# A fused graph network, linear attention and routed expert kernel on one Trainium2 core: the routed stage reads rows of sums, eight at a time, and its up product takes high and low halves side by side

## The reference

```
xn = _layernorm(x)
x  = x + gnn(xn, edges)                 # two graph convolutions, relu between
       + mix(xn)                        # linear attention over all nodes, projection, layer norm
x  = x + ffn(_layernorm(x))

def ffn(xt):                            # xt: 3125 x 768
    probs = softmax(xt @ router_w.T)    # 8 experts
    top_w, top_i = top_k(probs, 2)
    e_sel = max(top_i)                  # one expert for each row
    out = silu(xt @ W1[e_sel]) @ W2[e_sel]      # 768 -> 128 -> 768
```

## Time and profile before

| | us |
|---|---|
| median of 3 runs | 2436.15 (2434.61 to 2436.8) |
| the profiled execution's own time | 2431.91 |
| its span, first to last instruction | 2430.2 |
| PE busy in the span | 2332.9 (96%) |
| DVE, ACT, POOL busy | 1256.0, 865.0, 864.6 |

### The profile page before, as it was taken

The page is one execution under the profiler, slowest core; times in us unless marked ns, Lnnn a source line. Parts: engine busy times, 40 slices in busy tenths (PEclk is TensorE's granted clock), DMA queues, the critical chain, the costliest instruction groups (busy, mean ns, idle before and its releaser), DMA issues.

```text
span 2430.2 us, 44796 instructions
## 1 busy us (share of the span) xinstructions
PE 2332.9 (96%) x16783; PEld 1585.1 (65%) x16783; DVE 1256.0 (52%) x2843; ACT 865.0 (36%) x1323; POOL 864.6 (36%) x615
## 2 busy tenths in 40 slices
PE   5999999999999999999999999999999999999597
PEld 3878787878666666676666666666665566666375
DVE  6757575735667676765214344434431444444444
ACT  3546464634737373552113222222220111111143
POOL 1001216567777787776630111111100000000166
PEclk9999999999999999999999999999999999999899
DMA  7788876654332313234337867766745465554287
GB/s 287 276 282 286 264 274 156 180 130 81 66 64 3 66 0 65 19 34 111 47 55 235 241 208 210 232 216 205 220 167 198 146 216 182 190 189 152 76 180 141
DMA packets 172421, 385.63 MB, mean 159 GB/s; under 512 B 74800, under 2 KB 81818, under 8 KB 166396
## 3 DMA queue, kind: packets, MB, share of 16 engines
q1 hardware_dynamic: 90220, 313.83, 37.6%
q0 software_dynamic: 71264, 40.45, 15.4%
q10 hardware_dynamic: 10800, 29.50, 3.1%
HBM read 222.76 MB, written 166.44 MB: 160 GB/s over the span
## 4 chain that ended last, share of the span: by engine, by line
PE 79%; DVE 7%; ACT 7%; issue 4%; DMA 2%; SPq 1%; POOL 0%; DVEq 0%; ACTq 0%; POOLq 0%
PE pair L1899 33%; PE pair L393 31%; PE pair L1715 5%; PE pair L1695 2%; PE pair L1645 2%; DVE arena L1349 2%; DVE arena L1351 2%; DVE arena L1355 2%; ACT arena L950 2%; PE pair L1704 1%; ACT arena L879 1%; PE pair L1819 1%; DMA arena<-hl_dram,arena 1%; ACT arena L960 1%; ACT arena L886 1%
## 5 line engine op out<-in xcount | busy, mean ns | idle before, releaser
L393 PE MATMUL pair<-arena 128*128 128x384 f16 (+3 forms) x5760 | 894.4, 316 | 5.3 <-issue 3.4
L747 POOL DMA_INDIRECT cells<-arena x392 | 658.5, 1680 | 566.6 <-DMA cells<-arena 426.3
L1899 PE MATMUL pair<-arena 128*128 128x384 f16 x4900 | 814.2, 326 | 0.9 <-DVE arena L1516 0.9
L393 PEld LDWEIGHTS pair<-arena 128*128 128x128 f16 x5760 | 564.7, 98 | 318.0 <-issue 7.6
L1899 PEld LDWEIGHTS pair<-arena 128*128 128x128 f16 x4900 | 474.1, 98 | 306.8 <-issue 2.4
L779 POOL DMA_INDIRECT slots<-arena x25 | 28.8, 1150 | 484.7 <-DVEq L1571 452.1
L1715 PE MATMUL pair<-arena 128*128 128x66 f32 x1200 | 157.1, 274 | 4.2 <-ACT arena L921 3.9
L1715 PEld LDWEIGHTS pair<-arena 128*128 128x128 f32 x1200 | 145.9, 192 | 13.1 <-ACT arena L921 10.5
L921 ACT ACTIVATE arena<-pair,arena 128x256 f32<-128x256 f32 x300 | 124.0, 472 | 68.3 <-PE pair L1695 65.8
L1023 ACT ACTIVATE arena<-arena 128x768 f32<-128x768 f32 x25 | 23.4, 935 | 333.8 <-DVE arena L1450 333.8
L765 POOL DMA_DIRECT2D arena<-cells x25 | 30.3, 1213 | 284.7 <-DMA arena<-cells 278.1
(11 more groups left out here) (202 smaller groups left out, 2441.4 us busy)
## 6 DMA issues: line engine op xcount, KB each, us to landing
cells<-arena SPq DMA_DIRECT2D x50, 800.0 KB, 9.5
ahl_dram<-arena SPq DMA_DIRECT2D x23, 1600.0 KB, 10.9
arena<-ahl_dram SPq DMA_DIRECT2D x23, 1600.0 KB, 8.0
arena<-in_x SPq DMA_DIRECT2D x70, 384.0 KB, 3.8
arena<-key_dram SPq DMA_DIRECT2D x28, 896.0 KB, 5.7
arena<-cells SPq DMA_DIRECT2D x25, 800.0 KB, 7.5
arena<-cells POOLq DMA_DIRECT2D x25, 800.0 KB, 7.7
split_w<-arena SPq DMA_DIRECT2D x32, 384.0 KB
```

What stands on the lines that cost most here:

```text
L393: ins = nc.tensor.matmul(dst[half], left(k, a), right(k, b, half), start=start and n == 0, stop=stop and n == 2)
L747: nc.gpsimd.indirect_dma_start(cells[k], bass.IndirectOffsetOnAxis(ap=idx_all[:, m:m + 1], axis=0), val_all[:, m:m + 1], None, bounds_chec ...
L1899: ins = nc.tensor.matmul(pair[u][:, half, 0:HD], a[:, 0, s * P:(s + 1) * P], X[part][:, s, half * HD:(half + 1) * HD], start=(s == 0 and p ...
```

## The change

- `z_out` becomes 770 wide (`ZW`): the row of sums, then the shift and the scale of its layer norm. Layer 2 stores these rows to `z_rows` alone, in place of the store to the output and the one to `hl_dram`. The cast on ACT and `low` on DVE are gone.
- The router turns float32 rows: 6 float32 transposes with a float32 identity (`turn32`) in place of 12 float16 ones. ACT then copies the high halves out, and DVE subtracts them from PSUM for the low ones, behind ACT. The router of tile `T-2` is moved into the products of tile `T-1`.
- The routed stage gathers rows of sums (eight buffers), ACT normalises each with the shift and scale of its row (`rows_normal`), PE turns them in float32, ACT copies the high half out, and DVE subtracts (`rows_evict`).
- `up` has 6 products of 256 columns (high and low halves side by side, `fT`) and 6 of 128. The two halves of the result are added on DVE (`add_halves`) before silu reads them. `down` uses one pair of PSUM banks, so it waits for the result before it.
- The result is added to the gathered row on DVE and written to the output rows without adding in memory. A buffer of gathered rows is thus free only after the result.
- The table is made one tile a partition; PE reads 24 of the 32 expert numbers before the stage's first transposes (`READ_FIRST`). POOL clears the gather buffers before the last tile's slots.

```diff
-NG, NO = 6, 4
+NG, NO = 8, 4
+ZW = D + 2
+READ_FIRST = 24
...
             def layer2(n, u, i):
-                act.wait_ge(out_ev, n + 1)
-                act.dma_start(out[bass.ds(tile_at(n) * P, P), :], z_out[u]).then_inc(out_st[u], 16)
                 if reused(n):
                     route_evict(n - 1)
                 act.wait_ge(var_ready, C + n + 1)
                 nc.scalar.activation(lnb[:, u, 0:1], lnb[:, u, 1:2], ACT.Sqrt).then_inc(sd_ready, 1)
                 act.wait_ge(xn_ready, T + n + 1)
-                if reused(i):
-                    act.wait_ge(xn_st[u], 16 * (13 - u) + 16 * i)
-                    act.wait_ge(tr_done, n - 1)
-                nc.scalar.copy(fhl[u][:, 0:D], fn).then_inc(hi_ready, 1)
-                act.wait_ge(lo_ready, T + n + 1)
-                act.dma_start(hl_dram[bass.ds(tile_at(n) * P, P), :], fhl[u]).then_inc(xn_st[u], 16)
+                act.dma_start(z_rows[bass.ds(tile_at(n) * P, P), :], z_out[u]).then_inc(out_st[u], 16)
...
+            def rows_normal(j):
+                q = j % NG
+                act.wait_ge(gathered[q], gathered_base[q] + 16 * (j // NG) + 16)
+                if j >= 2:
+                    act.wait_ge(g_tr, j - 1)
+                nc.scalar.activation(gx[j % 2], g_in[q][:, 0:D], ACT.Identity, bias=g_in[q][:, D:D + 1],
+                                     scale=g_in[q][:, D + 1:D + 2]).then_inc(f_norm, 1)
...
             for j in range(FT):
+                if j + 3 < FT:
+                    rows_normal(j + 3)
                 if j + 2 < FT:
                     rows_evict(j + 2)
                 if j + 1 < FT:
                     silu(j + 1)
...
             def rows_evict(j):
-                dve.wait_ge(g_tr, j + 1)
-                nc.vector.tensor_copy(fT[1][j % 2], bank16(1)[:, 0:D]).then_inc(fT_lo, 1)
+                dve.wait_ge(fT_hi, j + 1)
+                nc.vector.tensor_tensor(fT[j % 2][:, :, 1, :], blocks(turned(j % 2)), fT[j % 2][:, :, 0, :], ALU.subtract)\
+                    .then_inc(fT_lo, 1)
+
+            def add_halves(j):
+                dve.wait_ge(f_h, j + 1)
+                nc.vector.tensor_copy(hsum[j % 2], bank(4 + j % 2)[:, 0:P]).then_inc(f_half, 1)
+                dve.wait_ge(f_half, f_half_base + j + 1)
+                nc.vector.tensor_tensor(hsum[j % 2], hsum[j % 2], bank(4 + j % 2)[:, P:2 * P], ALU.add).then_inc(f_sum, 1)
...
             for j in range(FT):
                 if j + 2 < FT:
                     rows_evict(j + 2)
                 if j + 1 < FT:
+                    add_halves(j + 1)
                     act_low(j + 1)
                 result(j)
...
+            def turn32(i, rows):
+                for k in range(K):
+                    ins = nc.tensor.transpose(turned(i)[:, k * P:(k + 1) * P], rows[:, k * P:(k + 1) * P], ident32)
+                return ins
...
-            for j in range(3):
+            for j in range(READ_FIRST):
                 read_expert(j)
             rows_turn(0)
             rows_turn(1)
```

More of the change, by code:

```diff
@@ L253, in build @@
         lnb = at(RT + 19104, 2, 16)
[L255 to L258, removed]
+        g_in = [at(RX + ZW * u, ZW) for u in range(NG)]
+        FR = RX + NG * ZW
+        fT = [at(FR + D * u, K, 2, P, dt=F16) for u in range(2)]
+        hsum = [at(FR + 2560 + NO * D + 2 * D + P * u, P) for u in range(2)]
+        blocks = lambda ap: ap.rearrange("p (k n) -> p k n", k=K)
         hact = [at(FR + 1536 + P * u, P) for u in range(2)]
@@ L262, in build @@
         fo = [at(FR + 2048 + D * u, D) for u in range(NO)]
-        reach, reach_n = at(FR + 2048 + NO * D, FT, NX), at(FR + 2304 + NO * D, FT, NX)
+        ident32 = at(WST, P)
+        gx = [at(FR + 2560 + NO * D + D * u, D) for u in range(2)]
         TAB = WST + 2304
@@ L479, in build @@
         table = sem("table")
[L480 to L483, removed]
+        gathered, g_tr = [sem(f"gathered{u}") for u in range(6)] + strip_added, sem("g_tr")
+        gathered_base = [0] * 6 + [16 * ((T + 1 - u) // 2) for u in range(2)]
+        fT_hi, fT_lo, f_h, f_act, f_ahi = [sem(f"f_{n}") for n in ("T_hi", "T_lo", "h", "act", "ahi")]
+        f_alo, f_alo_base, f_y, f_y_base = k_cast, UNITS, kp_full, UNITS * TC
+        f_half, f_half_base, f_sum, f_sum_base = k_low, 2 * UNITS, kp_exp, UNITS * TC + 2
+        f_out, added = sem("f_out"), [sem("added0"), sem("added1"), far_st, scattered[0]]
         added_base = [0] * 2 + [16, 16 * G * groups[0]]
@@ L777, in _ @@
             for n in range(T):
+                if n == T - 1:
+                    pool.wait_ge(g2_full, T)
+                    for u in range(NG):
+                        made.link(nc.gpsimd.memset(g_in[u], 0.0))
                 pool.wait_ge(f_slot, n + 1)
@@ L1515, in finish @@
                     dve.wait_ge(out_st[u], 16 * i)
[L1516 removed]
+                nc.vector.scalar_tensor_tensor(halves(z_out[u][:, 0:D]), wide(u), dinv[:, bass.ds(tile_at(n), 1)], halves(rl[u]),
                                                ALU.mult, ALU.add).then_inc(out_ev, 1)
@@ L1580, in layer2 @@
                     choose(n - 1)
-                normal(n, u)
+                normal(n, u, i)
                 if late:
                     place(n - 1)
-                low(n, u)
-            over_tiles(dve, layer2)
+            over_tiles(dve, layer2, T - 2)
+            layer2(T - 2, 1, T // 2 - 1)
+            route_evict(T - 2)
+            choose(T - 2)
+            place(T - 2)
+            finish(T - 1, 0, T // 2)
+            statistics2(T - 1, 0)
+            normal(T - 1, 0, T // 2)
             route_evict(T - 1)
@@ L1621, in result @@
             def result(j):
-                dve.wait_ge(f_y, j + 1)
+                dve.wait_ge(f_y, f_y_base + j + 1)
                 if j >= NO:
                     dve.wait_ge(added[j % NO], added_base[j % NO] + 16 * (j // NO))
-                nc.vector.tensor_copy(halves(fo[j % NO]), wide(2 + j % 2)).then_inc(f_out, 1)
+                nc.vector.tensor_tensor(halves(fo[j % NO]), wide(3), halves(g_in[j % NG][:, 0:D]), ALU.add)\
+                    .then_inc(f_out, 1)
             rows_evict(0)
             rows_evict(1)
+            add_halves(0)
             act_low(0)
@@ L1998, in layer2 @@
                         route_prefix(n - 2)
+                    if isinstance(n, int) and n == T - 1:
+                        if s == 14:
+                            route_turn(n - 1, 1 - u)
+                        if s == 18:
+                            route_logits(n - 1)
+                        if s == 23:
+                            route_prefix(n - 1)
                     if s == T - 1:
```

169 lines of the change are left out of this document (87 added, 82 removed).

## The result

| | before | after |
|---|---|---|
| median of 4 runs | 2436.18 us (2434.61 to 2436.8) | 2448.18 us (2445.84 to 2451.51) |
| ratio to before | 1 | 1.0053 [1.004, 1.0065] |
| profiled execution, own time | 2431.91 us | 2447.99 us |
| span | 2430.2 us | 2445.6 us |

By the two profiled executions the change costs 15.4 us of span.

What follows compares the result with a forecast made beforehand. The prediction took a closed ring of ACT and DVE to bound the changed routed stage. 0 + 2.3 + 21.6 - 1.2 = +22.7 us on 2431.91 gave 2454.6, plus 4.2 to the median: 2459 us, range 2449 to 2481.

Steps and rivals of the forecast that it cites:

- The ring: Routed stage: silu waits for DVE's add, behind the subtraction, which waits for ACT's copy; closed each round, 4.05 us.
- the round: Routed stage, per tile: pieces of 3.85 us plus seven hand-offs of 0.2 together, 4.05 us; 29 rounds 117.5 us.
- Lead-in and tail: Routed stage: 6.1 us before the rounds; after them 3.1 for one without normalising and 6.1 for the last results.
- The start: Last tile to first transposes: last slot 2.6 us earlier, but 24 reads (15.6 us) start PE 2.3 us later.
- The turns in layer 2: Router in layer 2: six float32 transposes at 0.11 us take 0.66 us, same as now, so 0 us.
- dear transposes: Rival: two records per float32 transpose, 0.22 us; +15 us in layer 2, 1 in the lead-in, 2475 us; chance 0.22.
- the cheap ones: Rival: float32 transposes at 0.055 us each, like float16, giving 2451 us; chance 0.06.
- The clock: Rival: PE's clock falls in the routed stage, rounds of 4.5 to 5.2 us, 2472 to 2492 us; chance 0.15.
- The end: Behind the last result, 9.9 us now: plain scatter 0.5 shorter and no queueing (0.7), -1.2 us.
- The sum: Whole kernel: 0 (turns) + 2.3 (start) + 21.6 (routed stage) - 1.2 (end) = +22.7 us.

Runs made afterwards that it cites:

- narrow_up: Changed kernel with up as 18 products of 128 columns, silu reading PSUM directly and no copy or add of halves on DVE; 2447.91 us, ratio 1.0048.
- narrow_spread: narrow_up with 19 of the 24 expert-number reads before the first two turns and 5 behind them; 2446.4 us, ratio 1.0041.
- narrow_half_turn: narrow_up with rows normalised to float16 and turned by six float16 transposes; 2443.29 us (one run).
- add_first_fixed: Changed kernel with DVE adding halves before the next subtraction, and up always using expert 0's weights at a fixed address; 2437.01 us (one run).
- the run with the halves first: Changed kernel with DVE adding the halves of round j+1 before it subtracts for round j+2; 2438.08 us, ratio 1.0013.

## Why the prediction was right, and where its sizes were off

**The direction and the mechanism hold, the size is half.** The ring is there with the order that the prediction gave, 1.54 us of waiting on ACT in each round (about 1.6 forecast), and two edits that touch only the ring shortened the round by 0.4 and 0.33 us. Work beside it left the round at 3.80 us: transposes doubled, `up` at fixed addresses. Two buffers less lengthened six rounds by 2.2 us in all in the trace, where the prediction had eight buffers gain nothing.

**The term that was mis-sized is the round: 3.80 us instead of 4.05.** Two of seven steps account for it. From the cast to the normalising behind it are 0.21 us where I took 0.30 + 0.03, and from the subtraction to the copy behind it 0.87 where I took 0.96 + 0.03. In both the next instruction stands on the same engine and waits for nothing else, and it starts some 0.1 us before the recorded end of the one ahead. I had added a hand-off there instead. The timeline of DVE in the kernel before had shown it, had I looked for two neighbours of which the second waits for nothing new: the second of these, behind DVE's last `finish`, starts 0.46 us behind the first, which lasts 0.55.

```profile
2281.73 0.55 DVE L1522 BATCH_NORM_STATS2 arena<-arena 128x6 f32<-128x384 f32 x1
2282.19 0.54 DVE L1523 BATCH_NORM_STATS2 arena<-arena 128x6 f32<-128x384 f32 x1
```

Over 29 rounds this is 7.3 us of the miss. Lead-in and tail were 1.6 longer than worked out, among other things because a turn at half clock takes 1.4 us (12 transposes 2.82). So the stage is 127.1 us against 132.8 forecast and 111.2 before: +15.9, not +21.6.

**The start** came out at -0.4 us instead of +2.3. By its parts: the last tile got 1.0 us longer (1.0 forecast), the chain from DVE's `finish` behind it to the last slot is 12.2 us (11.6 forecast, 15.2 before), the table follows 2.7 behind (2.9), and the reads take 15.7 (15.6). What I did not have is that layer 2 runs 3.0 us earlier in this trace; 1.6 of it stem from stages that the change does not touch. The other 1.4 come in layer 2, nearly all in its first tiles, where PE's first turn waits for DVE. Before, it waited 4.59 us, for `low` (L1540); now it waits 2.92, for the layer norm:

```profile
1888.90 1.46 PE L1645 MATMUL pair<-arena 128*128 128x128 f16 x12 [4.59 <-DVE arena L1540]
```

```profile
1885.63 1.54 PE L1686 MATMUL pair<-arena 128*128 128x128 f32 x6 [2.92 <-DVEq L1564]
```

The prediction had put the cast and `low` that leave layer 2 at nothing, since they run beside PE's products. At the first turn they do not. The 1.6 us from the other stages are chance, since nothing in the change acts there.

**The turns in layer 2** cost nothing, as forecast. Six float32 transposes, one record each, take 0.65 us from the first to the product behind them, 0.11 each:

```profile
2260.52 0.82 PE L1686 MATMUL pair<-arena 128*128 128x128 f32 x6
2261.17 1.14 PE L1940 MATMUL pair<-arena 128*128 128x384 f16 x6
```

That rules out the dear transposes and the cheap ones. The Trainium skill (TensorE: Matmul & The Clock Gate, Terms) has a float32 transpose four times faster than a product, which would be 0.33 us a turn if columns alone set the pace; the trace does not agree with that use of it. The prediction's own terms, from the rows of float32 products, gave the right 0.66.

**The clock** rose to 1.00 by 2318 us and stayed there to 2430, with six transposes and 18 products in each round and PE busy 92.10 of 114 us, so that rival is out for this kernel. By the Trainium skill (TensorE: Matmul & The Clock Gate, Part 4: PE-mode transpose) transposes do not count as work; the rounds here, which mix them with products, kept the clock all the same. In four of the kernels made from it (narrow_up, narrow_spread, narrow_half_turn, add_first_fixed) the clock did fall in the stage, two to five times, behind late starts.

**The end** is 9.8 us against 9.9, not 8.7. POOL's scatter did get shorter (1.02 us where the add took 1.6), and the end did not.

**The sum** is -0.4 + 15.9 - 0.1 = +15.4 us, the difference of the spans, against +22.7. The rest of the miss, some 3.5 us, is the step from the profiled execution to the median: before's lay 4.2 us below its median, and I added that to the forecast, while after's lies 0.2 below its own. One execution of before at the lower end of its scatter is no constant of the kernel.

**`up`** was worked out at 1.0 us from its columns and takes 1.64 in the run with the halves first. In the changed kernel what it takes is hidden behind the ring. With the ring open it counts: 0.64 us in each of 29 rounds are 19 us, about what the swap gave less than expected (10 us instead of 23 to 32). The wide form did not make `up` shorter than the 18 narrow products of the kernel before, which took 1.33 us in its round. The run with fixed addresses shows that the registers are a small part of it; the rest stays open.

## What to carry to other kernels

When work moves to engines that have time free, write down for one round who waits for whom in the order of each queue, and follow it until it closes: a ring through half-busy engines is a bound of its own, it is found by reading the queues and not from busy shares, and a swap of two calls or one instruction on another engine shortens it, until the next bound is reached. Size its steps from start to start between neighbours, with a hand-off only where an engine really waits. And behind the bound that is opened stands the next, so work out that one too before counting the gain: here it was `up`, sized by its columns at 1.0 us and measured at 1.64.

## What the runs showed of the hardware

- In the run with the halves first a product with its weights at a register's address started 0.125 us behind the one before, whether it had 256 or 128 columns; at a fixed address a pair of the two started in 0.165 us. In the changed kernel, where PE has waited before, the first pairs of a round also start 0.165 us apart with addresses from registers (2356.81 and 2356.98). The starts are not the pace of the results: at fixed addresses DVE's copy started 0.36 to 0.44 us behind the recorded end of `up` in rounds without a longer delay. Per address PE ran a register instruction of 46 ns. This is the view of line 2082 in the run with the halves first:

```profile
L2082 PEldq FUSED_REGOPS  x192: 46/46/70, 2312.6 to 2420.7; - x192
```

- On ACT and on DVE an instruction that waits for nothing started about 0.1 us before the recorded end of the one ahead (0.93 us behind a start of 1.02 us, 0.87 behind one of 0.96).
- A float32 transpose of 128 x 128 took 0.11 us from start to start at clock 1.00 and about 0.21 where twelve took 2.82 us at half clock.
- In the kernels in which PE runs ahead (the narrow ones, and fixed weights with the halves first) ACT and DVE start up to 4.0 us behind the recorded end of PE's products, with no other wait in the trace. PE's signals themselves are late there, and three that should have come over 1.8 us came within 0.15. In narrow_up PE also paused for 0.50 us within `up` at that time. Behind some of the longer of these delays, and nowhere else in the rounds, the granted clock fell to 0.50. The kernel before has no such start, though it reads `up` from PSUM in the same way. No run here tells why the signals are late.
